# A deformable convolution with four row blocks of five instead of two of nine, and its x hats made by spreading points on TensorE

## The reference

```python
def _dcnv4(t, H, W, Wv, bv, Wom, bom, Wo):
    value = (t @ Wv + bv).reshape(N, H, W, G, Cg)          # G = 4 groups of Cg = 8 channels
    om = (t @ Wom + bom).reshape(N, H, W, G, 3 * K)        # K = 9 taps
    offset = om[..., :2 * K].reshape(N, H, W, G, K, 2)
    mask = om[..., 2 * K:]
    loc_y = ys + ky + offset[..., 1]
    loc_x = xs + kx + offset[..., 0]
    sampled = _bilinear_gather(value, loc_y, loc_x)        # zero outside the picture
    out = (sampled * mask[..., None]).sum(axis=4)
    return out.reshape(N, L, C) @ Wo
...
t = _dcnv4(t, ...); y = relu(_bn(t)); t = _dcnv4(y, ...); y = _bn(t) + shortcut; conv1x1(y, Wc)
```

## Time and profile before

| | us |
|---|---|
| median of 3 runs | 520.45 |
| lowest, highest | 519.09, 524.11 |
| the profiled execution | 518.91 |
| its span, first to last instruction | 517.1 |
| mean granted clock of TensorE, of full speed | 0.952 |

### The profile page before, as it was taken

The page is one execution under the profiler, slowest core; times in us unless marked ns, Lnnn a source line. Parts: engine busy times, 40 slices in busy tenths (PEclk is TensorE's granted clock), DMA queues, the critical chain, the costliest instruction groups (busy, mean ns, idle before and its releaser), DMA issues.

```text
span 517.1 us, 10243 instructions
## 1 busy us (share of the span) xinstructions
PE 463.7 (90%) x3334; PEld 325.7 (63%) x3334; DVE 419.9 (81%) x998; ACT 302.2 (58%) x554; POOL 212.5 (41%) x168
## 2 busy tenths in 40 slices
PE   6979889999987759999999859999999899699785
PEld 5868523333346637777778637877777888455474
DVE  4978899998783498999999598999998586799551
ACT  3742448898744347777771277777760223798540
POOL 4004450000000078999984189999974031000000
PEclk9999899999999678999999969999999999899995
DMA  8700000000000000000000000000000000000000
GB/s 325 329 2 0 1 1 1 1 1 0 1 1 1 0 2 1 1 0 0 1 0 1 1 1 1 0 1 0 0 1 0 1 1 1 2 1 2 2 1 20
DMA packets 1475, 9.16 MB, mean 18 GB/s; under 512 B 160, under 2 KB 928, under 8 KB 1056
## 3 DMA queue, kind: packets, MB, share of 16 engines
q1 hardware_dynamic: 1296, 8.62, 4.2%
q10 hardware_dynamic: 144, 0.07, 0.1%
HBM read 8.43 MB, written 0.26 MB: 17 GB/s over the span
## 4 chain that ended last, share of the span: by engine, by line
PE 60%; DVE 20%; ACT 8%; issue 6%; POOL 4%; DMA 0%; DVEq 0%; SPq 0%; POOLq 0%
PE bank L1226 24%; PE bank L1171 13%; PE bank L1207 6%; ACT RINGS L555 3%; DVE RINGS L780 2%; PE bank L985 2%; PE bank L1312 2%; PE bank L1292 2%; PE bank L1176 2%; DVE SMT L859 1%; DVE PRD L850 1%; POOL RINGS L255 1%; POOL PR L276 1%; DVE PR L692 1%; DVE XN L623 1%
## 5 line engine op out<-in xcount | busy, mean ns | idle before, releaser
L1226 PE MATMUL bank<-VB,RINGS 128*128 (+1 forms) x576 | 159.6, 415 | 0.3
L255 POOL TENSOR_TENSOR RINGS<-LXA,cst 128x1152 f32<-128x1152 f32 x32 | 69.2, 2162 | 125.8 <-DVE LXA L831 125.8
L1226 PEld LDWEIGHTS bank<-VB,RINGS 128*128 128x128 f32 x576 | 104.5, 195 | 23.0 <-issue 1.8
L850 DVE TENSOR_TENSOR PRD<-bank,HYM 128x288 f32<-128x288 f32 x288 | 110.6, 448 | 8.4 <-PE bank L1226 3.7
L780 DVE TENSOR_SCALAR RINGS<-XP,wb 128x512 f32<-128x512 f32 x176 | 79.4, 527 | 7.9 <-PE bank L1171 6.6
L460 ACT ACTIVATE RINGS<-XP,wb 128x512 f32<-128x512 f32 x112 | 70.1, 712 | 16.9 <-PE bank L1171 16.8
L985 PE MATMUL bank<-cst 128*128 128x128 f32 x650 | 78.6, 281 | 0.0
L985 PEld LDWEIGHTS bank<-cst 128*128 128x128 f32 x650 | 77.5, 198 | 0.5
L1171 PE MATMUL bank<-RINGS,cst 128*32 128x512 f32 x576 | 74.4, 598 | 3.7 <-DVE RINGS L780 3.7
L324 POOL TENSOR_TENSOR PRD<-PRD 128x864 f32<-128x864 f32 x32 | 65.2, 2038 | 17.5 <-DVE PRD L850 17.5
L859 DVE TENSOR_REDUCE SMT<-PRD 128x1728 f32 (+1 forms) x32 | 62.1, 1941 | 0.1
(11 more groups left out here) (247 smaller groups left out, 519.6 us busy)
## 6 DMA issues: line engine op xcount, KB each, us to landing
wb<-in_wb SPq DMA_DIRECT2D x1, 3068.5 KB, 12.3
wd<-in_wd SPq DMA_DIRECT2D x1, 2729.5 KB, 20.8
wc<-in_wc SPq DMA_DIRECT2D x1, 1255.0 KB, 14.9
cst<-in_cst SPq DMA_DIRECT2D x1, 645.0 KB, 5.4
XC<-in_x SPq DMA_DIRECT2D x2, 128.0 KB, 2.4
out_y<-XC SPq DMA_DIRECT2D x2, 128.0 KB, 1.8
wa<-in_wa SPq DMA_DIRECT2D x1, 209.0 KB, 5.5
cst<-in_cst ACTq DMA_DIRECT2D x1, 66.0 KB, 2.7
```

The costliest lines, as they stand in the source:

```text
L255: pool.tensor_tensor(view(DXY, o, [[WW, KG * NA], [1, WW]]), view(LXA, n * KG * NA, [[1, KG * NA], [0, WW]]), view(cst, CST["xg"], [[0, KG ...
L850: dve.tensor_tensor(view(PRD, (half * K9 + k) * 288, [[72, G], [NR, CG], [1, NR]]), view(bank[2 + (9 * half + k) % LOOK], 0, [[72, G], [NR ...
L1226: pe.matmul(bank[2 + (9 * half + k) % LOOK][:, 0:288], view(HXT, (half * K9 + k) * P, [[1, P]]), view(VB, b * 288, [[1, 288]]), start=True ...
```

## The change

`NA` = 4 blocks of `NR` = 5 rows (0 to 4, 4 to 8, 8 to 12, 12 to 15). The groups are taken two at a time (`GP` = 2 pairs): the 128 partitions of a tile of hats are now 2 groups x 4 blocks x 16 columns, and the moving `VB` of a product is 2 groups' 8 channels x 5 rows = 80 columns (`COLS`). An image has 36 products, in six units of six (`products`), where it had 18.

The x hats are no longer computed with pixels on the partitions and then transposed. For each image the points' lx for all blocks (`LXA`, 96 numbers a pixel for each pair: three "quads" of 3 taps x 2 groups x 4 blocks, with padding) are transposed instead (`turn_points`, 4 transposes), copied out by ACT (`points_out`), and spread over the 16 columns by nine matmuls with a 0/1 matrix of 32 rows, "select" (`spread`, three to a call, on row groups 0, 1 and 2 of the array and into three banks). ACT takes |. - x| from the bank (`distances_x`, nine of 512), and POOL makes min(. - 1, 0), which is minus the hat (`hats`, nine of 512); the sign is taken back at the end of the turn. The result is already in the layout that `products` reads. The y hats are made per image (`rows_off`, `rows_hat`, `masked`). POOL's `pairs` are gone, and `sums` reduces all 1440 products of a half. `sample` handles 480 elements, six times an image. The loops are written out. `products` alternate between banks 0 and 1; the other six banks are two trios for the spread.

```diff
-NA, NR = 2, 9
+NA, NR = 4, 5
+GP = G // 2
 PADW = HH + 2
 KG = K9 * G
-HXN, HYN = KG * NA * WW, KG * NR
-HATS = HXN + HYN
+TAPS2 = GP * K9
+COLS = 2 * CG * NR
+HYN = KG * NR
+PRN = TAPS2 * COLS
+HXN = K9 * 512
+LXW = 96
...
-LOOK = 6
-PAIRS = 3
...
+    def rows_off(turn, b):
+        i = B * turn + b
+        pool.wait_ge(lxa_ready, pointed(turn, b))
+        after(pool, prod_used, 6 * (i - 1))
+        pool.tensor_tensor(view(HY, b % 2 * 2 * HYN, [[NR, 2 * KG], [1, NR]]),
+                           view(LY, b * 2 * KG, [[1, 2 * KG], [0, NR]]),
+                           view(cst, CST["yg"], [[0, 2 * KG], [1, NR]]), ALU.subtract).then_inc(dy_ready, 1)
+    def masked(turn, b):
+        pool.wait_ge(hy_ready, B * turn + b + 1)
+        hy = view(HY, b % 2 * 2 * HYN, [[NR, 2 * KG], [1, NR]])
+        pool.tensor_tensor(hy, hy, view(MM, b * 2 * KG, [[1, 2 * KG], [0, NR]]), ALU.mult).then_inc(hym_ready, 1)
+    def hats(turn, b, j):
+        i = B * turn + b
+        for quad in range(3):
+            pool.wait_ge(abs_done, 9 * i + 3 * j + quad + 1)
+            hx = view(HX, b % 2 * HXN + (3 * quad + j) * 512, [[1, 512]])
+            pool.tensor_scalar(hx, hx, 1.0, 0.0, ALU.subtract, ALU.min).then_inc(hat_ready, 1)
...
     for turn in range(2):
-        for half in range(2):
-            pool.wait_ge(lxa_ready, 3 * turn + half + 1)
-            distances(turn, 0, half)
-        def pairs(b, half):
-            n = 2 * b + half
-            pool.wait_ge(prod_used, 9 * (16 * turn + n) + 2 * PAIRS)
-            first, second = (view(PRD, (half * K9 + k) * 288, [[1, PAIRS * 288]]) for k in (0, PAIRS))
-            pool.tensor_tensor(second, second, first, ALU.add).then_inc(paired, 1)
-        def body(b, ahead):
-            masked(turn, b, 1)
-            if ahead >= 1:
-                distances(turn, b + 1, 1)
-            pairs(b, 0)
-            if ahead >= 1:
-                masked(turn, b + 1, 0)
-            if ahead == 2:
-                distances(turn, b + 2, 0)
-            pairs(b, 1)
-        masked(turn, 0, 0)
-        distances(turn, 1, 0)
-        body(0, 2)
-        body(1, 2)
-        pool.wait_ge(lxa_ready, 3 * turn + 3)
-        with pool.Fori(2, B - 2) as b:
-            body(b, 2)
-        body(B - 2, 1)
-        body(B - 1, 0)
-    pool.wait_ge(prod_done, 2 * 16 * K9)
+        rows_off(turn, 0)
+        for b in range(B):
+            hats(turn, b, 0)
+            masked(turn, b)
+            hats(turn, b, 1)
+            if b + 1 < B:
+                rows_off(turn, b + 1)
+            hats(turn, b, 2)
...
+    def points_out(i):
+        act.wait_ge(t_done, i + 1)
+        after(act, sel_done, 9 * i)
+        act.activation(view(LXT, 0, [[1, 512]], n=LXW), bank[trio(i, 0)][0:LXW, :], ACT.Copy).then_inc(lxt_ready, 1)
+    def rows_hat(i):
+        hy = view(HY, i % 2 * 2 * HYN, [[1, 2 * HYN]])
+        act.wait_ge(dy_ready, i + 1)
+        act.activation(hy, hy, ACT.Abs).then_inc(hy_abs, 1)
+        act.wait_ge(hy_abs, i + 1)
+        act.activation(hy, hy, ACT.Relu, scale=-1.0, bias=cv("one", 1)).then_inc(hy_ready, 1)
+    def distances_x(i, j):
+        after(act, prod_done, 6 * (i - 1))
+        for quad in range(3):
+            act.wait_ge(sel_done, 9 * i + 3 * j + quad + 1)
+            act.activation(view(HX, i % 2 * HXN + (3 * quad + j) * 512, [[1, 512]]), bank[trio(i, j) + quad][:, :],
+                           ACT.Abs, bias=cv("mx", 1)).then_inc(abs_done, 1)
...
+        for b in range(B):
+            i = B * turn + b
+            points_out(i)
+            rows_hat(i)
+            for j in range(3):
+                distances_x(i, j)
...
+    def points(b, count):
+        at, n = b * 2 * KG, count * 2 * KG
+        flat = lambda t: view(t, at, [[1, n]])
+        sixes = lambda t: view(t, at, [[6, n // 6], [1, 6]])
+        link(dve.tensor_scalar(flat(AM), flat(LY), 4.0, None, ALU.is_ge))
+        link(dve.scalar_tensor_tensor(flat(AM), flat(LY), 8.0, flat(AM), ALU.is_ge, ALU.add))
+        link(dve.scalar_tensor_tensor(flat(AM), flat(LY), 12.0, flat(AM), ALU.is_ge, ALU.add))
+        link(dve.scalar_tensor_tensor(flat(LY), flat(AM), -4.0, flat(LY), ALU.mult, ALU.add))
+        link(dve.tensor_scalar(flat(AM), flat(AM), FAR, None, ALU.mult))
+        for a in range(NA):
+            ins = dve.scalar_tensor_tensor(view(LXA, b * 2 * GP * LXW + a, [[32, n // 6], [NA, 6]]), sixes(AM), -a * FAR,
+                                           sixes(LX), ALU.add, ALU.add)
+        ins.then_inc(lxa_ready, 1)
...
+    def sample(i, half, part):
+        q = 6 * i + 3 * half + part
+        dve.wait_ge(hym_ready, i + 1)
+        after(dve, smp_ready, 2 * i + half - 1)
+        dve.wait_ge(prod_done, q + 1)
+        dims = [[COLS, 6], [2 * NR, CG], [1, 2 * NR]]
+        dve.tensor_tensor(view(PRD, half * PRN + part * 6 * COLS, dims), view(bank[q % 2], 0, dims),
+                          view(HY, (i % 2 * 2 + half) * HYN + part * 12 * NR, [[2 * NR, 6], [0, CG], [1, 2 * NR]]),
+                          ALU.mult).then_inc(prod_used, 1)
+    def sums(i, half):
+        bh, b4 = divmod(i % B, B4)
+        dve.wait_ge(prod_used, 6 * i + 3 * half + 3)
+        dve.tensor_reduce(view(SMT, bh * NPIX + half * P + b4 * C, [[C // GP, GP], [1, C // GP]]),
+                          view(PRD, half * PRN, [[K9 * COLS, GP], [NR, C // GP], [COLS, K9], [1, NR]]), AX.XY,
                           ALU.add).then_inc(smp_ready, 1)
...
     def deform(turn):
+        offsets(turn, 0, 0)
+        offsets(turn, 0, 1)
+        points(0, 1)
         if turn == 0:
+            dve.wait_ge(vb_clear, 3)
         values(turn, 0)
         values(turn, 1)
+        offsets(turn, 1, 0)
+        offsets(turn, 1, 1)
+        points(1, B4 - 1)
+        for b in range(B):
+            i = B * turn + b
+            sample(i, 0, 0)
+            if b:
+                sums(i - 1, 1)
+            sample(i, 0, 1)
+            sample(i, 0, 2)
+            sample(i, 1, 0)
+            sums(i, 0)
+            if b == 1:
+                points(B4, B4)
+            sample(i, 1, 1)
+            sample(i, 1, 2)
+        sums(B * turn + B - 1, 1)
...
+    def turn_points(turn, b):
+        i = B * turn + b
+        pe.wait_ge(lxa_ready, pointed(turn, b))
+        after(pe, abs_done, 9 * i - 3)
+        for u in range(2 * GP):
+            ins = pe.transpose(bank[trio(i, 0)][0:LXW, u * P:(u + 1) * P], view(LXA, (b * 2 * GP + u) * LXW, [[1, LXW]]), ident)
+        ins.then_inc(t_done, 1)
+    def spread(turn, b, j):
+        i = B * turn + b
+        pe.wait_ge(lxt_ready, i + 1)
+        after(pe, abs_done, 9 * i + 3 * j - 3)
+        if b == 0 and j == 1:
+            pe.wait_ge(val_used, NBH * (turn + 1))
+        for quad in range(3):
+            pe.matmul(bank[trio(i, j) + quad][:, :], cv("select", P, j * P, 32 * quad, 32),
+                      view(LXT, 0, [[1, 512]], 32 * quad, 32), start=True, stop=True).then_inc(sel_done, 1)
+    def products(turn, b, half, part):
+        i = B * turn + b
+        q = 6 * i + 3 * half + part
+        if half == part == 0:
+            pe.wait_ge(hat_ready, 9 * (i + 1))
+            if b == 0:
+                pe.wait_ge(om_used, 4 * turn + 4)
+                pe.wait_ge(val_used, NBH * (turn + 1))
+        after(pe, prod_used, q - 1)
+        for e in range(6 * part, 6 * part + 6):
+            gp, k = divmod(e, K9)
+            ins = pe.matmul(bank[q % 2][:, e % 6 * COLS:(e % 6 + 1) * COLS],
+                            view(HX, b % 2 * HXN + k * 512 + (half * GP + gp) * P, [[1, P]]),
+                            view(VB, (b * GP + gp) * COLS, [[1, COLS]]), start=True, stop=True, skip_group_check=True)
+        ins.then_inc(prod_done, 1)
...
+        turn_points(turn, 0)
+        for j in range(3):
+            spread(turn, 0, j)
+        for b in range(B):
+            ahead = b + 1 < B
+            if ahead:
+                turn_points(turn, b + 1)
+            for u in range(6):
+                products(turn, b, *divmod(u, 3))
+                if ahead and u < 3:
+                    spread(turn, b + 1, u)
+        keep_warm(bank[7], FILL_TAIL)
...
```

251 lines of the change are left out of this document (68 added, 183 removed).

## The result

The changed kernel takes 815.96 us (median of 4 runs, 814.52 to 816.94) against 519.77 us (median of 4, 518.92 to 524.11): a ratio of 1.567, 95% interval 1.558 to 1.576. It is 296 us slower. I had forecast 594 us, 75 slower, with a range up to 628. The sign was right and the size was off by a factor of four.

What follows compares the result with a forecast made beforehand. TensorE was taken to set the pace, VectorE hardly less busy. A call: 17.5 + 6 x 16.7 + 11.2 + 8.0 + 2.5 + 4.4 = 143.8 us; two calls add 75.3 to 518.9, giving 594 us, range 553 to 628.

Steps and rivals of the forecast that it cites:

- to the first product: Set-up of a call, with early hats on POOL and points on DVE: 17.5 us, 14 to 21 possible.
- six images with the wait, and the points: Images 1 to 6 wait 4.3 us for POOL's hats, 16.7 us each; points of images 4 to 7 add 4.4.
- image 6: Stretch from image 6 to 7, without the wait because no further `rows_off` follows: 11.2 us.
- image 7: Last image of a call, products only, with nothing to spread: 8.0 us.
- to the transposes of `SMT`: End of a call after the last product: matmul drain 0.16, `sample` 0.65, reduction 1.6, together 2.5 us.
- the second case: Trace window 443.5 to 446.9, after short attention bursts with gaps: clock at 0.50 for 3.4 us only, TensorE busy for 3.17.
- the rival of 623 us: Low clock lasts 10.2 us, slowing three units and three spreads: 3.6 in place of 1.2 us, 12 times; chance 0.08.
- signs of being wrong: Forecast wrong if hats come ahead of need, loads start 0.07 us apart, or the clock stays low through the loop.
- The hat on POOL: A `tensor_scalar` of 512 on POOL, taken as 0.8 us between a memset's 0.51 and a two-input addition's 1.26.
- The points on DVE: In image 1, points of images 4 to 7 stand ahead of two `sample`: 4.4 us, all on the path.
- the rival of 559 us: Products' weight loads are faster in a stream, 81 ns for load and matmul: 35 us less; faster loads 0.07.
- the break-even of 10.5: Time per image at which the change decides between faster and slower: 10.5 us, from a call's 106.1 us before.

Runs made afterwards that it cites:

- the fastest variant: Changed kernel with hats on ScalarE, 112 columns moving, useless matmuls filling set-up gaps, and 8 in place of 22 at the loop's end: 568.81 us, ratio 1.093.

## Why the prediction was right and wrong

The terms of one call, predicted and measured (182.04, 208.68, 412.88, 428.53 and 435.51 of the timeline, and 389.32, where the chain of waits has the first product of image 6):

| us | predicted | measured |
|---|---|---|
| to the first product | 17.5 | 26.6 |
| six images with the wait, and the points | 6 x 16.7 + 4.4 = 104.6 | 180.6 |
| image 6 | 11.2 | 23.6 |
| image 7 | 8.0 | 15.7 |
| to the transposes of `SMT` | 2.5 | 7.0 |
| sum | 143.8 | 253.5 |

**The step that failed is the clock's**: "What follows the wait here is dense work, as in the second case, so I take 3.4 us at the lower level per image." The lower level lasted the whole loop. My longest case, the rival of 623 us, had it for 10.2 us and took for granted that it ends; a clock that stays low through the loop stood among my signs of being wrong, but without a price. Hats on ScalarE showed that it doesn't end even without any wait; 112 columns, that it ends when the products are wider; both together, that most of the loss goes with it. The filled wait showed the other side: once up, the clock stayed up through images of 80 columns and fell only behind idle time. So the wait takes the clock down, as I had it, and what failed is the recovery. I argued from the row of 443.5 to 446.9 as if any busy TensorE were alike. The attention's matmuls behind it move 256 columns for loads of 32 rows, and the products here move 80 behind a load of 128x128. The row came from another mix of matmuls, and no row of this mix was in the trace; that should have put a case with the whole loop at the lower level among the rivals, and its price into the range.

**The price at the lower level was wrong too.** I took 0.133 us for a record there, because I let the load's 0.111 stand and only the columns slow down. At the lower level the 36 records of the chain took 7.91 us, 0.220 each; at the higher level, in the run with the wait filled, 0.113. It isn't the columns that double it: a unit at the lower level took 2.85 us with 80 columns and 2.90 with 112. The load's pace follows the granted clock. The Trainium skill, "TensorE: Matmul & The Clock Gate", section "LDWEIGHTS (loading the stationary operand)", gives the number of columns over 1.2 GHz as a load's time, without regard to the level; the trace agrees at the higher level and not at the lower one, where it is twice that. Together the two errors on the clock are, per image, 16.3 - 8.0 on the products and 6.0 - 3.2 on the spreads, less the 1.2 that I had: 9.9 of the 13.1 us by which an image was off.

**The hat on POOL was mis-sized**: 0.8 us taken, 1.93 measured, outside my bounds of 0.51 and 1.26. Three of them are 5.7 us in place of 2.4, the other 3.3 of the 13.1. The ranking by the number of inputs was the error; two operations with immediates cost more than an addition of two tensors. The Trainium skill, "GPSIMD Engine Reference", section 3.1, has 769 ns for 512 elements in the best loop; by it I would have been as far off, since a hat here took 2.5 times that best case.

**Set-up and end.** The set-up took 9.1 us more, since POOL's nine hats stand nearly in a row there (5.98, 5.68 and 5.69 us for three each in its timeline, in place of 2.4). The 16.8 us of before that I leaned on lead to the first `sample`; its first product came after 12.6. The end took 4.5 more: the 44 records of `keep_warm` run at the lower level until 433 and last 7.36 us, longer than the reduction that they were to cover; with 8 matmuls in place of 22 and the clock up, the transposes come 2.6 us after the last product's end, as forecast. Image 7 is the clock's alone; image 6 is the clock's too, and 1.2 us of waiting for its successor's last hats. The points on DVE were over-estimated: image 1 took 31.6 us against 29.8 for its neighbours, 1.8 and not 4.4. In the fastest variant, with quick units, the gap is 4.09 us; that slow products cover the rest in the changed kernel is my reading of the two, no run tested it.

**Right** were the order of the wait and its other links (1.75 us between last product and hats, predicted 1.9), DVE's prices (0.657 and 1.643 us; 0.65 and 1.6 predicted), the weight load as the pace of a product (0.113 at the higher level; this settles the rival of 559 us against the 81 ns), and the overlap of three row groups (a spread of three in 1.07 us; 1.06 predicted). So was the count that the loads leave nothing to gain: even with the wait gone and the clock up an image takes 13.1 us, over the break-even of 10.5. My 11.2 lacked 0.6 for the transposes and 0.6 for ACT's copy of the points, which only the wait had hidden, and 0.7 for the rest, by my reading mostly changes of shape.

By the runs, the two causes that I mis-sized make 234 of the 296 us, 247 with the gaps of the set-up filled as well, and TensorE's own work, the points on DVE and the set-up the remaining 48. How the 234 is shared between clock and hats has no single answer, because the hats' gap is one of the two things that hold the clock down.

## What to carry to other kernels

When matmuls get narrower behind full weight loads, price them at the lower level of the clock as well, and look for a row in which that very mix runs; a stretch of another shape that recovered is no evidence. Before an elementwise step is moved to POOL, find a row of the same form there, or let ScalarE do it: the number of inputs was no guide to its price here. If a wait is to be filled to hold the clock, the fill must cover it at the higher level too: one that ended 3.4 us early lost it every time. Where a profile has both a gap and a low clock, take each cause away by itself and then both; here they gave 103 and 76 us alone and 234 together.
